# One attention and mixture-of-experts layer: which probability chunks are transposed by DMA and which on TensorE, and three steps moved in their queues

## The reference

```python
xn = layernorm(x)                                   # x: 2 x 2048 x 256
# attention, one head of 256
scores = ((xn @ W_qk) @ xn.T) / 16 + (kpos - qpos) * slope      # causal
s = softmax(scores) @ (xn @ W_v.T)
# mixture of 8 experts, top 1, 512 slots each, first come first kept
p, e = max(softmax(xn @ Wr))
y = p * (relu(xn @ W1[e]) @ W2[e])                  # 256 -> 1024 -> 256, 0 if no slot
out = x + s * silu(y)
```

## Time and profile before

| | before |
|---|---|
| median of 3 runs | 440.85 us (440.56 to 442.42) |
| profiled execution | 440.56 us, span 438.8 us |
| PE busy | 420.2 us, 96% of the span |
| DVE busy | 323.6 us, 74% |
| ACT busy | 221.7 us, 51% |
| POOL busy | 231.0 us, 53% |
| granted TensorE clock | 1.000 |

### The profile page before, as it was taken

One profiled execution on the slowest core, in us unless ns is written; L12 is line 12 of the kernel. 1 busy time (PEld: TensorE's weight loads), 2 busy tenths in 40 slices (PEclk: granted clock), 3 DMA queues, 4 the chain that ended last, 5 costly groups with the idle time before them and its releaser, 6 DMA issues.

```text
span 438.8 us, 8377 instructions
## 1 busy us (share of the span) xinstructions
PE 420.2 (96%) x3022; PEld 287.7 (66%) x3022; DVE 323.6 (74%) x839; ACT 221.7 (51%) x436; POOL 231.0 (53%) x360
## 2 busy tenths in 40 slices
PE   5799899997999899999999999999999999999996
PEld 2367576675678677676766666666666666665676
DVE  5989778988898568778758797979696966424563
ACT  1756365353655246645435554545454545454551
POOL 5337870834726735146202666575757575757530
PEclk9999999999999999999999999999999999999999
DMA  7992749465955643266746577676778773244850
GB/s 235 357 374 68 218 133 226 94 127 109 298 149 98 103 165 71 77 229 170 143 48 253 183 232 240 196 261 184 264 174 266 178 202 92 93 119 115 154 104 30
DMA packets 99928, 74.96 MB, mean 171 GB/s; under 512 B 68911, under 2 KB 93756, under 8 KB 97840
## 3 DMA queue, kind: packets, MB, share of 16 engines
q1 hardware_dynamic: 88624, 52.06, 45.6%
q0 software_dynamic: 5824, 16.74, 12.7%
q10 hardware_dynamic: 5440, 5.64, 4.0%
HBM read 31.33 MB, written 28.58 MB: 137 GB/s over the span
## 4 chain that ended last, share of the span: by engine, by line
PE 73%; DVE 13%; DMA 5%; ACT 4%; issue 3%; POOL 0%; another core or an unknown queue 0%; ACTq 0%; SPq 0%; DVEq 0%
PE bank L1350 19%; PE bank L1352 19%; PE bank L1351 19%; PE bank L1439 4%; PE bank L1442 4%; PE bank L1441 4%; DMA pT<-p_rows 4%; DVE sc L975 3%; PE bank L1420 3%; DVE p_rows L996 2%; ACT sc L1224 2%; DVE stats L823 1%; DMA xg<-in_x 1%; DVE pT L996 1%; DVE w_l L1047 1%
## 5 line engine op out<-in xcount | busy, mean ns | idle before, releaser
L1439 PE MATMUL bank<-v_h,pT 128*128 128x257 f16 x272 | 74.6, 274 | 3.3 <-DMA pT<-p_rows 3.2
L1442 PE MATMUL bank<-v_h,pT 128*128 128x257 f16 x272 | 74.1, 272 | 0.0
L1441 PE MATMUL bank<-v_l,pT 128*128 128x256 f16 x272 | 73.7, 271 | 0.0
L1251 ACT ACTIVATE hid_h<-bank 128x512 f16<-128x512 f32 x64 | 38.0, 594 | 67.2 <-PE bank L1352 61.3
L1065 DVE SCALAR_TENSOR_TENSOR hid_l<-bank,hid_h 128x512 f16<-128x512 f32 x64 | 43.9, 685 | 37.8 <-ACT hid_h L1251 35.4
L1351 PE MATMUL bank<-w_l,hid_h 128*128 128x256 f16 x256 | 69.8, 273 | 0.0
L1350 PE MATMUL bank<-w_h,hid_h 128*128 128x256 f16 x256 | 69.8, 273 | 0.0
L1352 PE MATMUL bank<-w_h,hid_l 128*128 128x256 f16 x256 | 69.8, 273 | 0.0
L975 DVE CUSTOM_DVE_ANT_0 sc<-bank,bias,score_mul 128x512 f32<-128x512 f32 (+2 forms) x80 | 52.9, 664 | 9.6 <-PE bank L1352 9.3
L1350 PE MATMUL bank<-xT,qT_h 128*128 128x512 f16 (+3 forms) x160 | 55.0, 347 | 2.7 <-DVE cmin L975 2.4
L1351 PE MATMUL bank<-xT,qT_h 128*128 128x512 f16 (+3 forms) x160 | 55.1, 347 | 0.0
(11 more groups left out here) (183 smaller groups left out, 917.1 us busy)
## 6 DMA issues: line engine op xcount, KB each, us to landing
raw<-in_w_e SPq DMA_DIRECT2D x5, 2048.0 KB
sc<-in_w_e SPq DMA_DIRECT2D x3, 2048.0 KB
slots<-empty ACTq DMA_DIRECT2D x1, 4224.0 KB, 20.1
gates<-gate SPq DMA_DIRECT2D x8, 512.0 KB
out<-xg SPq DMA_DIRECT2D x7, 512.0 KB
rows<-xg SPq DMA_DIRECT2D x7, 512.0 KB, 7.0
rows<-so SPq DMA_DIRECT2D x7, 512.0 KB
xg<-in_x SPq DMA_DIRECT2D x6, 512.0 KB, 4.9
```

The source lines that it names most:

```text
L1251: a_.activation(hid_h[:, f % HB, :], sc_ps[f % 2][:, :], ACT.Relu).then_inc(h_hi, 1)
L1439: pe.matmul(pv_ps[t % 2][:, 0:D + 1], p_h, v_h[:, at, q, 0:D + 1], start=kb == 0, stop=False)
L1441: pe.matmul(pv_ps[t % 2][:, 0:D], p_h, v_l[:, at, q, :], start=False, stop=False)
L1442: last = pe.matmul(pv_ps[t % 2][:, 0:D + 1], p_l, v_h[:, at, q, 0:D + 1], start=False, stop=kb == t % NT)
```

## The change

`by_dma` gets another table. Before, chunks 0 and 1 of tiles with three chunks, 1 and 2 of tiles 12 to 14, 1 of tile 15, and 0 to 2 of tiles 28 to 30 went by DMA, and none of tiles 27 and 31. Now it is chunk 1 of tiles with three chunks (but tile 27) and chunks 1 and 2 of every tile with four. `group_in(5)` moves ahead of the chunk transposes of tile 13 on SP. `scale(0, 0)` moves from step 2 of tile 12 to step 1, and the scaling of `last_g` on DVE from behind tile 30 to behind tile 29.

```diff
@@ by_dma
-            if t in (REST - 1, TILES - 1):
+            if t == REST - 1:
                 return False
-            if chunks(t) == 4:
-                return c == 1 if t == NT - 1 else c in ((1, 2) if t < NT else (0, 1, 2))
-            return chunks(t) == 3 and c < 2
+            return c in {3: (1,), 4: (1, 2)}.get(chunks(t), ())
@@ SP
                 if t == SPLIT_TILE[NG + 1]:
                     group_out(NG + 1)
+                    group_in(NG + 1)
                 for c in steps(t):
                     if by_dma(t, c):
                         chunk_turn(t, c)
-                if t == SPLIT_TILE[NG + 1]:
-                    group_in(NG + 1)
@@ DVE, between
-                if (t, c) == (FIRST_SCALE, 2):
+                if (t, c) == (FIRST_SCALE, 1):
                     scale(0, 0)
@@ DVE, tiles from REST
                 tile(t)
-                if t == REST + 2:
+                if t == REST + 1:
```

## The result

| | before | after |
|---|---|---|
| median of 5 runs, taken side by side | 442.02 us | 446.22 us |
| lowest and highest of them | 440.56, 442.63 | 445.28, 446.86 |
| ratio of after to before | | 1.010, 95% interval 1.0085 to 1.0115 |
| profiled execution | 440.56 us | 445.72 us |
| its span | 438.8 us | 444.0 us |

What follows compares the result with a forecast made beforehand. From tile 8 on PE was taken as the bound, with 6.0 us of holes. To the profiled 440.56 us came +1.0 (to tile 16), +1.3 (tiles 24 to 26) and +2.4 (last stage): 445.3 us, range 441.0 to 448.5.

Steps and rivals of the forecast that it cites:

- three terms of the sum: Added PE time: +1.0 us at the end of tile 16, +1.3 in tiles 24 to 26, +2.4 in the last stage.
- The price of a turn: Four 128x128 transposes of a chunk on PE cost 0.44 us; net seven more chunks, +3.1 us of PE.
- Tiles 8 to 12: Four turns add 1.76 us, the 1.97 us hole goes, the 0.50 us hole keeps 0.4: net -0.3 us.
- The scale: Moved behind (12, 1), DVE waits 2.5 us for the weights' maxima; new PE hole of 1.1 us at score (14, 0).
- Tiles 15 and 16: One turn less, -0.44 us, but PE waits for DMA of (15, 1) and (15, 2): +1.0 us at tile 16's end.
- it keeps the +0.8: DVE sets the issue of the (15, 1) transfer and keeps the +0.8 us of lateness from the scale part.
- The reload of x: Moved on SP ahead of tile 13's transposes: cost 0, or 0.6 to 2 us if its wait is 9.3 us.
- rival C: Worse: reload wait long, transposes (13, 1) and (15, 2) late, DVE stalls spread; about 449 us, chance 0.12.
- Tiles 24 to 26: Three turns on PE with no hole of PE that they could close: +1.3 us.
- The last stage: Scaling of last_g waits for gathers, 2.3 us lost at score (31, 2); DMA of (31, 1) +1.3: +2.4 us.
- A: Broadcast and gathers land before DVE comes, or PE has enough lead, so waits are covered: 442.3 us, chance 0.20.
- B: Faster: only PE's work counts and every hole closes, 3.1 - 4.26 - 1.87 = -3.1: 437.5 us, chance 0.06.

Runs made afterwards that it cites:

- table-only run: Changed kernel with the scale, the scaling of last_g and the reload of x back in their old places, only by_dma's new table kept: 443.91 us, ratio 1.0046.
- the scale alone: Kernel before with only the scale of the first expert weights moved from behind (12, 2) to behind (12, 1): 442.62 us, ratio 1.0039.
- (11, 0) with and without the pieces: Kernel before with chunk (11, 0) turned on PE: ratio 0.9993; also with five expert-weight split pieces moved from tiles 13-15 to 17-19: 0.9996.
- the run with the scaling back: Changed kernel with only the scaling of last_g back behind tile 30: 445.12 us, ratio 1.0079.
- the one with its pieces moved: Changed kernel with five pieces of the expert-weight split moved from tiles 13 to 15 to tiles 17 to 19: 446.03 us, ratio 1.0089.
- (11, 0) with the pieces moved: Kernel before with chunk (11, 0) turned on PE and five expert-weight split pieces moved from tiles 13-15 to 17-19: 442.20 us, ratio 0.9996.
- the scaling alone: Kernel before with only the scaling of last_g moved from behind tile 30 to behind tile 29: 444.94 us, ratio 1.0073.

## Why the prediction was right, point by point

The time (446.22 us, or 445.72 for the profiled execution, for 445.3) and the sign were right. That the time came so near is in part luck. Of the three terms of the sum, the first was half of what it measured, the last nearly twice, and the two errors cancel: 1.0, 1.3 and 2.4 us were forecast, 2.0 (2.2 with 0.15 at the count near 190), 1.6 and 1.4 measured.

- **The price of a turn** (0.44 us a chunk): right. The steps of the account at (9, 1), (10, 1), (11, 1), (12, 1), (25, 1), (27, 1), (29, 1) and (31, 1) are 0.43 to 0.45 us. The Trainium skill (TensorE: Matmul & The Clock Gate, Part 4: PE-mode transpose) gives about 275 ns for one 128x128 transpose in a kernel, by which a turn of four would be 1.1 us, an estimate. As the duration of a single one the trace agrees (0.30 us at 145.02), but four overlap, and the steps don't bear the 1.1 us out.
- **Tiles 8 to 12** (-0.3): PE was at -0.85, since the hole of 0.50 us closed too. It was worth nothing in the changed kernel, since DVE was late behind it.
- **The scale**: both sizes came as forecast, DVE's idle time 2.48 us for 2.5, the hole at (14, 0) 0.97 us for 1.1. Each is a difference of two times that were both put too late: the maxima landed 0.7 us later than before and not 1.7, DVE came 0.3 us later and not 1.2; the read of (13, 2) was over at 112.9 and not at 113.7, PE would have come at 112.0 and not at 112.6. The step that failed is the sentence after it, "After this part PE is -0.3 + 1.1 = +0.8 us": it closes the account of tiles 13 to 15 with PE's place at (14, 0) and lets PE run at its pace from there. DVE was 1.97 us late at that time. The table-only run and the run of the scale alone show the two halves, 0.98 and 0.97 us at (18, 0), and together 1.95 of the 2.04 us. (Taking the scale back from the changed kernel gave only 0.42 us of it, since the load for group 4 came 0.6 us later in that trace.) I had put DVE's slip at 1.3 us in tiles 8 to 11 and then used it only for one hole. And these rows of the kernel before, which the prediction did not use, say where DVE had room to make good: stretch and its length, busy time of PE, PE's weight loads, DVE, ScalarE and POOL, PE's clock, DMA share, GB/s.

```profile
112.00:118.00 6.00, 6.00 (x41) 3.87 (x40) 4.18 (x11) 5.19 (x10) 4.06 (x12) 1.00 1.23 244
118.00:124.00 6.00, 6.00 (x48) 4.48 (x46) 5.93 (x12) 2.30 (x4) 1.96 (x2) 1.00 0.98 312
124.00:130.00 6.00, 6.00 (x44) 4.14 (x43) 5.01 (x18) 5.49 (x13) 1.68 (x2) 1.00 0.54 134
130.00:136.00 6.00, 6.00 (x46) 4.20 (x45) 5.89 (x16) 1.56 (x4) 5.68 (x7) 1.00 0.26 51
```

From 112 to 118 it had room (4.18 of 6.00 us), and it did make good there: 0.7 us of its lateness between score (13, 3) and the half of (13, 0), in the changed kernel, with the table only and with the scale alone, until it met the late load for group 4. From 118 on it had less: 5.93, 5.01 and 5.89 of 6.00 us. PE is full all along, so PE's timeline alone shows one bound where there were two, and neither shows the third, SP's queue.
- **Tiles 15 and 16**: "The hole only becomes longer" was wrong for (15, 1). Its transfer left at 144.16, 1.98 us later than before as DVE's half did, but was there no more than 3.1 us after that and not 4.51, and the hole at its values shrank from 1.61 to 0.12 us. The wait that the forecast put at 0.1 to 1.3 us came instead, at the values of (15, 2): 1.54 us, 3.2 us after the issue at 146.88. In the table-only run the two are 0.84 and 0.82 us. The 0.44 us of the turn that is gone went into a longer wait before the turn of (15, 3) (0.61 us for 0.18). In sum nothing more comes of these tiles than the 2.04 us that DVE had brought: "it keeps the +0.8" was right for the issue, with the wrong lateness in it.
- **The reload of x** (0, bounds 0.6 to 2): 0, by the run that undoes it. The reason was another than I gave. The walk had the transfer of (13, 1) there by 128, a microsecond before PE; it came at about 129.9, and PE, 1.3 us late through DVE, still waited for it. For an earlier PE it would have been some 1.8 us late, by the one trace above. This wait in tile 14 was the sign that was to lead to rival C, and the time did not go there.
- **Tiles 24 to 26** (+1.3): 1.58 us; the step at (26, 1) was 0.70 us instead of 0.44.
- **The last stage** (+2.4): 1.4 us. The walk was right in its order: scaling behind the gathers, one read of a score behind it, PE at (31, 2) behind that, then the transfer of (31, 1) (1.05 us for 1.3). Its size hung on a time of landing. These rows of the changed kernel answer to the earlier trace rows:

```profile
419.26 1.00 POOL L788 DMA_INDIRECT so<-gates,slot_idx  x1 [0.30 <-issue]
```
```profile
421.96 0.49 DVE L1160 TENSOR_SCALAR so<-so,value_mul 128x512 f32<-128x512 f32 x1 [4.02 <-DMA so<-gates,slot_idx]
422.01 1.02 POOL L797 TENSOR_TENSOR so<-so 128x256 f32<-128x256 f32 x1 [1.75 <-DMA so<-gates,slot_idx]
```

The issue moved, about with the rest of the kernel, by 4.08 us (from 415.18), but the gathers were there 2.70 us after it, where I had taken the 3.95 us of before. The kernel as a whole was 3.77 us late at this stage and the gathers only 2.83 us: this is the 0.9 us by which the hole is smaller (1.39 for 2.3). "POOL's work isn't touched" was true and no reason for a fixed landing.

**The rivals.** A, that the waits are covered: no, both are in the trace. Undone singly they gave back 1.0 and 1.1 us by the medians, with intervals that overlap that of the changed kernel; added singly to the kernel before, each made it slower, with the whole interval above 1. What A got right is that undoing both leaves a loss of only 0.5%. B, that holes closed stay closed: only as long as PE doesn't catch up with DVE, by the traces of (11, 0) with and without the pieces. Its sum was also off by 0.1: the holes of the last stage are 0.56 + 0.46 + 0.75 = 1.77 us and not 1.87. And of the 0.18 us "early in tile 16", the distance of the start at 145.02 from the one before it, only 0.07 us are hole. C, that the stalls of DVE spread to further holes: they did, but as one lateness of 2 us taken over once, not as the stall of SP that it was priced by.

Open stays why tiles 24 to 26 took 0.3 us beyond the turns. The table-only run took 2.0 us by its ratio of 1.0046 and 2.3 us by the medians, while its account (1.0 us to tile 18, 1.6 in tiles 24 to 26, 0.1 at the count, nothing net in the last stage by the run with the scaling back) adds up to 2.7 us. The interval covers the difference.

## What to carry to other kernels

Where two engines are both near full, keep an account for each of them: what counts at a point of the program is the later of the two, and a hole closed on one can be given back at the next place where it meets the other (here 1.24 of 1.96 us). A wait put on the second engine costs what is left of it at the meeting, some tiles behind (here 1.0 of 2.26 us), even where the first shows no wait at its place. What is left can hang on a third queue: here DVE had made 0.7 us of its lateness good when a load that SP had issued late, behind late transposes, brought it back. A wait moved ahead of work that used to be done while it ran adds that work, too: here one score's read and its half went from before the maxima to behind them.

## What the runs showed that I had not expected

The same transfers take very different times from trace to trace, also between kernels whose last stage is the same. From the issue of the last gather to the first instruction that waits for it there were 2.7 us in five traces (the changed kernel, the three in which one step of it was undone, and the one with its pieces moved), 2.9 to 3.5 us in five, 4.0 us before, and 4.6 to 4.9 us in three (table only, (11, 0) with the pieces moved, the scaling alone). The table-only run and the one with the scaling back have the same last stage, and 4.6 and 2.7 us. A transposed chunk of the last stage that landed late cost PE 1.4 us in one trace (the scaling alone) and 1.2 us in another ((11, 0) with the pieces moved), before any step that was moved there. What sets these times stays open; each kernel has one trace. So a wait for such a transfer with no lead has no single price but a spread of about 2 us, and, where PE stood 3.95 us behind it, the 1.5 us of the lower clock on top. A step behind it belongs as late as the program allows.
